# Between attention and experts: the order of the last two token tiles' routing, of the plan and of the first expert tiles

## The reference

```
h = tokenizer(x)                                   # 4 images x 256 tokens x 192
h = concatenate([h, txt])                          # 4 x 384 tokens x 192 = 1536 tokens
h = h + attention(layernorm(h))                    # softmax(-|q_n - q_m|^2 / 4) v, 12 heads, all 1536 x 1536
x = layernorm(h)
t = x / sqrt(mean(x*x) + eps) * norm_scale
g = t @ gate_w.T + gate_b                          # 16 logits for each token
top_vals, top_idx = top_k(g, 4)
comb = onehot(top_idx) weighted by softmax(top_vals)
u = t @ mlp1_w[e].T + mlp1_b[e]                    # 768 wide, pairs (glu, lin)
a = min(u_glu, 7) * sigmoid(1.702 * min(u_glu, 7)) * (clip(u_lin, -7, 7) + 1)
y = a @ mlp2_w[e].T + mlp2_b[e]
out = h + x + sum over the 4 experts of comb[e] * y[e]
```

## Time and profile before

| | |
|---|---|
| median of 3 runs | 739.37 us (733.47, 739.37, 743.79) |
| the profiled execution | 738.72 us |
| its span in the profile | 737.0 us |
| TensorE clock granted, mean of the span | 0.94 |
| busy: PE / PEld / DVE / ACT / POOL | 634.6 / 428.6 / 429.7 / 379.7 / 356.2 us |
| attention stage, about | 237 to 461 us |
| seam that the change touches, about | 461 to 498 us |
| expert stage, about | 489 to 724 us |

### The profile page before, as it was taken

The page is one execution under the profiler, slowest core; times in us unless marked ns, Lnnn a source line. Parts: engine busy times, 40 slices in busy tenths (PEclk is TensorE's granted clock), DMA queues, the critical chain, the costliest instruction groups (busy, mean ns, idle before and its releaser), DMA issues.

```text
span 737.0 us, 17256 instructions
## 1 busy us (share of the span) xinstructions
PE 634.6 (86%) x4926; PEld 428.6 (58%) x4927; DVE 429.7 (58%) x1430; ACT 379.7 (52%) x721; POOL 356.2 (48%) x401
## 2 busy tenths in 40 slices
PE   5888899888884999899999998549999999999970
PEld 5775786677641223222222223438999999999970
DVE  0347767676664235555555554537777777777750
ACT  0323438343312999988999898014344344344330
POOL 3112233222232125555555545514777787787781
PEclk9999999999985999999999999559999999999995
DMA  8999999400014426545555231059898999999834
GB/s 325 409 353 303 328 313 333 164 1 1 23 53 112 68 115 192 154 143 140 150 153 150 58 71 58 37 191 300 214 249 230 229 252 235 232 255 231 228 64 77
DMA packets 78192, 132.61 MB, mean 180 GB/s; under 512 B 36859, under 2 KB 62892, under 8 KB 76876
## 3 DMA queue, kind: packets, MB, share of 16 engines
q1 hardware_dynamic: 64892, 116.79, 50.7%
q0 software_dynamic: 11712, 14.19, 11.7%
q10 hardware_dynamic: 1552, 1.18, 0.5%
HBM read 105.53 MB, written 58.42 MB: 222 GB/s over the span
## 4 chain that ended last, share of the span: by engine, by line
PE 58%; DVE 10%; ACT 9%; DMA 8%; issue 6%; POOL 6%; another core or an unknown queue 1%; SPq 1%; ACTq 0%; DVEq 0%; POOLq 0%
PE ps L864 11%; PE ps L1015 9%; PE ps L851 9%; PE ps L1044 6%; PE ps L1025 5%; DMA odd_sum<-mid 4%; ACT big L1137 3%; ACT mid L1137 3%; PE ps L701 2%; PE ps L710 2%; POOL rstd L492 2%; DVE stat L1225 1%; DVE mid L1233 1%; PE ps L786 1%; DMA out<-mid 1%
## 5 line engine op out<-in xcount | busy, mean ns | idle before, releaser
L1137 ACT ACTIVATE mid<-ps 128x1536 f32<-128x1536 f32 x108 | 152.6, 1457 | 27.1 <-PE ps L851 26.3
L627 POOL TENSOR_TENSOR mid<-mid 128x384 f32<-128x384 f32 x63 | 81.2, 1289 | 53.2 <-DVE mid L1563 23.8
L851 PE MATMUL ps<-mid 52*128 52x512 f16 x432 | 88.0, 396 | 20.7 <-ACT big L1137 8.5
L1015 PE MATMUL ps<-mid,big 128*128 128x128 f32 x756 | 99.3, 282 | 0.3 <-ACT mid L1163 0.3
L1015 PEld LDWEIGHTS ps<-mid,big 128*128 128x128 f32 x756 | 91.5, 194 | 4.6 <-ACT mid L1163 0.5
L1554 DVE TENSOR_SCALAR mid<-ps,big 128x128 f32<-128x128 f32 x189 | 54.6, 344 | 62.0 <-PE ps L1025 34.7
L864 PE MATMUL ps<-mid 128*32 128x384 f32 x864 | 87.3, 507 | 0.0
L1170 ACT ACTIVATE mid<-mid 128x384 f32<-128x384 f32 x63 | 32.9, 522 | 88.4 <-DVE mid L1554 74.6
L1044 PE MATMUL ps<-big,mid 128*128 x378 | 71.0, 332 | 4.6 <-POOL mid L627 3.9
L851 PEld LDWEIGHTS ps<-mid 52*128 52x128 f16 x432 | 17.1, 95 | 85.8 <-ACT mid L1137 46.1
L1044 PEld LDWEIGHTS ps<-big,mid 128*128 128x128 f32 x378 | 60.1, 190 | 9.8 <-issue 9.6
(11 more groups left out here) (224 smaller groups left out, 1108.6 us busy)
## 6 DMA issues: line engine op xcount, KB each, us to landing
big<-w_cat SPq DMA_DIRECT2D x63, 576.0 KB
expert_in<-expert_in SPq DMA_DIRECT2D x16, 1774.5 KB, 48.4
big<-expert_in SPq DMA_DIRECT2D x63, 136.5 KB
w_cat<-w_a SPq DMA_DIRECT2D x4, 1536.0 KB, 7.6
big<-w SPq DMA_DIRECT2D x2, 2304.0 KB, 8.9
big<-patches SPq DMA_DIRECT2D x8, 512.0 KB, 8.8
big<-patches SPq DMA_DIRECT2D x2, 2048.0 KB, 21.9
w_cat<-w_b SPq DMA_DIRECT2D x2, 1536.0 KB, 7.5
```

What stands on the lines that cost most here:

```text
L627: nc.gpsimd.tensor_tensor(actv[r], prod[r], sig[r], ALU.mult).then_inc(actv_ready, 1)
L851: last = nc.tensor.matmul(SETS[kb % 2][:, c * 512:(c + 1) * 512], keysT[n_par][row:row + STK, kb * P:(kb + 1) * P], qrysT[n_par][row:row + ...
L1015: last = nc.tensor.matmul(banks[half][:, c * P:(c + 1) * P], w1_t[q][:, half * FF + c * P:half * FF + (c + 1) * P], xtT[r][:, 0:P], start= ...
L1137: nc.scalar.activation(probs[kb % 4], SETS[kb % 2], ACT.Exp, scale=0.5).then_inc(probs_ready, 1)
```

## The change

It touches only the order of things, and one job that is joined to another.

- DVE: `output(11)` comes before `weigh(10)`, and `norm_stats(11)` before `place(10)`.
- POOL: `route2` is split into `root_var` and `root_ms`. For the last two tiles: `root_var(11)`, the first scatter of tile 10, `root_ms(11)`, the scatters 1 and 2, `weights(11)`, the last scatter of tile 10, `base_add(11)`, the scatters of tile 11. Before, all four scatters stood between `route2(11)` and `weights(11)`.
- PE and DVE: the separate `counts` job is gone. The ranks job of tile 11 also computes the counts (as the seen tokens before tile 11 plus the mask of tile 11) beside the ranks in bank 7, and `place(11)` copies them out. All later job numbers are one lower.
- PE: `ranks(11)` comes before `weighted_bias(2)`; the plan's transposes come before `weighted_bias(4)` and `weighted_bias(5)`.
- SP: after the scatters have landed it issues rows 0, rows 1, weights 1, rows 2, weights 2, rows 3, weights 3; before, rows 0, weights 1, rows 1, weights 2, rows 2, weights 3, rows 3. Weights 0 go ahead of the wait in both.
- PE: the first products of tile 0 come before the transpose of tile 1.

```diff
             load_weights(0, 0)
             for k in range(2):
                 sp.wait_ge(rows_out[k], 16 * (TOPK * NT // 2 + 1))
-            for j in range(NW):
+            load_rows(0, 0)
+            for j in range(1, NW):
                 load_rows(j, j)
-                if j + 1 < NW:
-                    load_weights(j + 1, j + 1)
+                load_weights(j, j)
...
-            def route2(r):
+            def root_var(r):
                 held_wait(pool, lmv_ready, r + 1)
...
+            def root_ms(r):
                 held_wait(pool, ms_ready, r + 1)
...
-            def scatter(r, par):
+            def scatter(r, par, ks=range(TOPK)):
...
             weights(NT - 2)
             route(NT - 1)
-            route2(NT - 1)
-            scatter(NT - 2, 0)
+            root_var(NT - 1)
+            scatter(NT - 2, 0, (0,))
+            root_ms(NT - 1)
+            scatter(NT - 2, 0, (1, 2))
             weights(NT - 1)
+            scatter(NT - 2, 0, (3,))
             base_add(NT - 1)
             scatter(NT - 1, 1)
...
-            def ranks(r, job):
+            def ranks(r, job, counts=False):
...
-                nc.tensor.matmul(b7[:, 0:E], ones16[:], seen[:], start=False, stop=True).then_inc(tr_ready, 1)
-
-            def counts(job):
-
-                pe.wait_ge(tr_taken, job)
-                pe.wait_ge(slots_ready, NT)
-                nc.tensor.matmul(b7[:, 0:E], ones16[:], seen[:], start=True, stop=True).then_inc(tr_ready, 1)
+                last = nc.tensor.matmul(b7[:, 0:E], ones16[:], seen[:], start=False, stop=True)
+                if counts:
+                    nc.tensor.matmul(b7[:, E:2 * E], ones16[:], mask[:], start=True, stop=False)
+                    last = nc.tensor.matmul(b7[:, E:2 * E], ones16[:], seen[:], start=False, stop=True)
+                last.then_inc(tr_ready, 1)
...
             logits(base + 2)
+            ranks(NT - 1, base + 3, counts=True)
             weighted_bias(2)
-            ranks(NT - 1, base + 3)
             weighted_bias(3)
-            counts(base + 4)
+            pe.wait_ge(slots_ready, NT)
             for t in (NT - 2, NT - 1):
                 last = nc.tensor.transpose(ps[0:E, t * P:(t + 1) * P], comb_all[:, t, :], ident[:])
             last.then_inc(combT_psum, 1)
-            weighted_bias(4)
-            pe.wait_ge(combT_ready, 2)
-            weighted_bias(5)
-
-            pe.wait_ge(tr_taken, base + 5)
+            pe.wait_ge(tr_taken, base + 4)
             pe.wait_ge(plan_cols_ready, 1)
             for c in range(2):
                 last = nc.tensor.matmul(b7[0:1, c * P:(c + 1) * P], plan_cols[:, c:c + 1], ident[:], start=True, stop=True)
             last.then_inc(tr_ready, 1)
 
+            weighted_bias(4)
+            pe.wait_ge(combT_ready, 2)
+            weighted_bias(5)
+
...
             x_transpose(0, 0, 16)
+            mlp1(0, 0, 16)
             x_transpose(1, 1, 16)
-            two_tiles(0, 0, 0)
+            mlp1(1, 1, 16, narrow_first=True)
+            x_transpose(2, 2, 16)
+            x_transpose(3, 3, 16)
             two_tiles(2, 2, 0)
...
-            def place(r, par, job):
+            def place(r, par, job, counts=False):
 
                 dve.wait_ge(tr_ready, job + 1)
-                nc.vector.tensor_tensor(slot_e[:], b7[:, 0:E], bucket0[:], ALU.add).then_inc(tr_taken, 1)
+                last = nc.vector.tensor_tensor(slot_e[:], b7[:, 0:E], bucket0[:], ALU.add)
+                if counts:
+                    last = nc.vector.tensor_copy(cnt, b7[:, E:2 * E])
+                last.then_inc(tr_taken, 1)
...
             choose(NT - 2, base + 5)
-            weigh(NT - 2, 0)
             base += 7
             output(NT - 1, base - 1)
+            weigh(NT - 2, 0)
+            norm_stats(NT - 1, 1)
             place(NT - 2, 0, base)
-            norm_stats(NT - 1, 1)
             norm_square(NT - 1, 1)
...
-            place(NT - 1, 1, base + 3)
+            place(NT - 1, 1, base + 3, counts=True)
             dve.wait_ge(slots_ready, NT)
-
-            dve.wait_ge(tr_ready, base + 5)
-            nc.vector.tensor_copy(cnt, b7[:, 0:E]).then_inc(tr_taken, 1)
-            dve.wait_ge(tr_taken, base + 5)
             dve.wait_ge(plan_consts, 1)
```

More of the change, by code:

```diff
@@ L565, in weights @@
                 nc.gpsimd.tensor_tensor(wexp[:], euler[:], gd[:], ALU.pow).then_inc(wexp_ready, 1)
-            def scatter(r, par):
+            def scatter(r, par, ks=range(TOPK)):
                 held_wait(pool, slots_ready, r + 1)
-                for k in range(TOPK):
+                for k in ks:
                     nc.gpsimd.indirect_dma_start(
@@ L583, in pool_head @@
                 route(n - 1)
-                route2(n - 1)
+                root_var(n - 1)
+                root_ms(n - 1)
                 base_add(n - 1)
@@ L607, in _ @@
             weights(NT - 3)
-            route2(NT - 2)
+            root_var(NT - 2)
+            root_ms(NT - 2)
             base_add(NT - 2)
@@ L989, in _ @@
             last.then_inc(tr_ready, 1)
+            weighted_bias(4)
+            pe.wait_ge(combT_ready, 2)
+            weighted_bias(5)
             pe.wait_ge(w_in, 16 * 2)
             pe.wait_ge(plan_ready, 1)
-            pe.wait_ge(tr_taken, base + 6)
+            pe.wait_ge(tr_taken, base + 5)
             pe.wait_ge(bias_added, NT // 2)
@@ L1532, in _ @@
                                            ALU.add).then_inc(plan_cols_ready, 1)
-            dve.wait_ge(tr_ready, base + 6)
+            dve.wait_ge(tr_ready, base + 5)
             nc.vector.tensor_copy(ej_i, b7[0:1, 0:MT])
@@ L1536, in _ @@
             nc.vector.tensor_scalar(exrow_i, b7[0:1, 0:MT], float(P), None, ALU.mult).then_inc(tr_taken, 1)
-            dve.wait_ge(tr_taken, base + 6)
+            dve.wait_ge(tr_taken, base + 5)
             nc.vector.tensor_copy(bank_mark[:], ones[:, 0:1]).then_inc(plan_ready, 1)
```

## The result

The changed kernel takes 734.93 us (median of 20 runs, 730.38 to 741.98), the kernel before 740.74 (20 runs, 732.86 to 748.02). The ratio is 0.9947, 95% interval 0.9921 to 0.9972: about 3.9 us shorter, somewhere between 2 and 6. It is formed from the fast runs and is the measure used from here on; the two medians themselves lie 5.8 us apart, near the far end of that range. The forecast was 735.0 and 4.2 us.

The account below looks back on a forecast made before the run. TensorE bounds the later expert stage; the change shortens the wait chain ahead, about 460 to 500 us. Tile 1's products end 4.4 earlier, or 3.7; the sum is given as 4.2, so 735 us, range 729.5 to 741.5.

Parts of the forecast that it names:

- Output before weighing, roots and scatters: VectorE and GpSimd around tiles 10 and 11: the row of tile 11 is written from 467.1 instead of 467.94, 0.8 earlier.
- The 0.39 charged for a stall: Weighing tile 10 on VectorE: its first product is stretched under GpSimd's h_res add, from 0.23 to 0.62.
- the wider reading: Contention rule taken to cover scatters too: the square at 465.3 waits 0.9 for the first scatter; sum 0.8 smaller.
- I charge scatters nothing: VectorE beside GpSimd's scatters: GpSimd adds stretch two-input products, but scatters are given no cost.
- The power: GpSimd's power of tile 11, formerly behind four scatters of tile 10: runs from 470.7 instead of 473.14, 2.4 earlier.
- the scatters' landing: DMA of tile 11's four scatters: follows the slots rigidly and lands at 481.7 instead of 484.18.
- The plan: Plan and first weight issue come 3.4 earlier, at 479.9; no gain by itself, as SP waits for scatters until 481.7.
- Row load 0: First row load, issued by SP at 482.5: takes 3.2 (bounds 2.5 to 3.9), landing at 485.7.
- Products of tile 0: TensorE, ahead of tile 1's transpose: start at 486.9 instead of 492.03; tile 1's products end 4.4 earlier, or 3.7.
- Rival B: Part is given back: half clock through tile 1 (+1.9) or row loads gain nothing; 2.3 remain, 736.5; chance 0.20.
- The DMA of h_res ... shifts with it: ScalarE's transfer of h_res into out, awaited by GpSimd's first add: issued behind copy 3 and shifts with it.
- The conveyor: Later expert stage, TensorE busy 99.91 of 100 us at full clock: an earlier first tile should make the end earlier.

Follow-up runs that it names:

- plan_only: The kernel before with only the counts inside the ranks job and the plan's transposes ahead of the last bias products; ratio to before 0.9983 (0.9949 to 1.0018).
- start_only: The kernel before with only the new order of loads and tile 0's products ahead of tile 1's transpose; ratio to before 0.9975 (0.9946 to 1.0005).
- undo_sp: The changed kernel with the old order of loads (weights 1 ahead of rows 1, and so on); ratio to before 0.9968 (0.9930 to 1.0006).
- slots_only: The kernel before with only VectorE's new order and tile 10's scatters in pieces around the two powers; ratio to before 0.9957 (0.9924 to 0.9989).
- gate_loose: The changed kernel with GpSimd's product of tile 3 ahead of the first indirect add, later products likewise; ratio to before 0.9948 (0.9909 to 0.9986).
- gate_old_start: The changed kernel with GpSimd's product of tile 3 ahead of the first add and both start edits taken back; ratio to before 0.9951 (0.9915 to 0.9987).
- undo_pe: The changed kernel with TensorE's old start order, transposes of tiles 0 and 1 before tile 0's products; ratio to before 0.9982 (0.9946 to 1.0018).
- warm: The changed kernel with 11 unread products on TensorE behind the last bias products, before the first rows; ratio to before 0.9995 (0.9951 to 1.0040).
- out_mid: The changed kernel with the h_res transfer issued behind ScalarE's copies of tiles 0 and 1; ratio to before 0.9944 (0.9902 to 0.9986).

## Why the prediction was right

The time, its sign and its size were right. Step by step, counted from the last output copy:

- **Output before weighing, roots and scatters:** the row of tile 11 was forecast 0.8 earlier and came 1.3 earlier (8.1 to 6.8). The 0.39 charged for a stall didn't occur: VectorE's product began at 458.33, GpSimd's add at 458.43, and the product took 0.22. The Trainium skill's "SBUF — State Buffer", section "Who interferes with whom", says that issue order decides which of the two blocks; the trace agrees as far as the product, 0.1 ahead, wasn't held, while the add behind it took 0.59, as in the earlier trace rows, so that it was blocked can't be seen. The square at 461.50 took 0.36 inside the scatter of 461.26 to 462.42, as before (466.24), so the wider reading doesn't hold for it. But "I charge scatters nothing" was too simple: one step of weighing, L1467, took 0.48 at 468.72, inside the scatter of 468.19 to 469.23, and took 0.23 before; in all eleven kernels with the new slots it took 0.48 there. What singles it out among VectorE's steps beside scatters is open. What I charged for the held root, 0.1 to 0.3, was 0.14 (its input stood at 462.32 with the usual 0.08, it began 462.46).
- **The power,** the largest term: 2.4 forecast, 2.9 measured (13.3 to 10.4); **slots** 2.5 and 2.9; **the scatters' landing** 2.5 and 3.3 (24.4 to 21.1), as the last piece landed in 2.91 and not 3.21. The stall of placing under the base add was small (0.33 for 0.22), where up to 0.39 was charged.
- **The plan** earlier gains nothing on its own: right for the issue of row load 0, which in `plan_only` is where it was.
- **Row load 0** lands in 2.8 (478.44 to 481.25); I took 3.2.
- **Products of tile 0:** 5.1 forecast, 6.4 measured, but tile 0 takes 4.5 and not 3.5, and the pause 1.1 and not 0.7, since the products of tile 0 and the transpose behind them lie at half clock: tile 1's end 4.4 forecast, 4.1 measured. Rival B's half clock through tile 1 did not come here; it came in `start_only` and `undo_sp`.
- **"The DMA of h_res ... shifts with it"** is the term that was wrong. It was issued 4.3 earlier and took 1.0 longer, beside loads that were themselves brought forward, and tile 3's product waits for it. At tile 4 the lead was 4.5, at tile 6 3.3; against the end of tile 1 it is 0.8 lost.
- **The conveyor,** on which an earlier first tile makes an earlier end, held for these two kernels (222.7 and 222.6 from tile 6 on). Over all fourteen profiles that stretch differed by up to 4.7.

So the sum of 4.2 (the working gives 4.4, or 3.7 with a slower load, and doesn't say how it comes to 4.2) is near 3.4 (profile) and 3.9 (runs) because terms that were too small and others that were too large cancel, and that is luck. The mechanism of the slots was right. What the sum got wrong is who earned it. It put 1.9 of the 4.4 at tile 1's end on the start edits (2.5 on the slots); `slots_only` alone has tile 6 at 50.9, the whole change at 51.2. In the whole change the lead of the start edits is spent on the half clock and on the h_res gate. That this is all they are ever worth is not shown: `gate_loose` against `gate_old_start` leaves them 1.4.

## What to carry to other kernels

Between two stages, move the issue of a slow queue behind the small operation that others wait for: four scatters, 1.27 to 1.53 us apart, stood ahead of one power, and the reordering around them had as much as the whole change. When the first operations of the next stage are brought forward, look for the next wait that all of them share (here a transfer whose landing one engine's order puts ahead of another's work), and count what moves forward with it on the same DMA engines. An earlier start with a pause in it can bring less than nothing at tile 2 (`start_only`: 2.9 ahead at tile 0, 0.8 behind at tile 2, at half clock throughout), and an idle 2 us later on costs its own length and then some half clock (`undo_pe`, `warm`). And when one wait is taken away, look at what binds next before counting the gain: `out_mid` and `gate_loose` open the gate in two ways, and both stop at tile 6 at 49.5.

## What was not expected of the hardware

- From the first product on the half clock lasted 9.2 us in `start_only` and 8.9 in `undo_sp`, both with one pause of 1.1 us between products of which 0.47 is idle, and 4.5 to 5.2 us in the five other profiles with that pause. Without it it was 2.6 to 3.4 in four profiles (`slots_only`, `undo_pe`, before, `plan_only`) and 5.2 in `gate_old_start`. So the pause goes with a longer half clock in these profiles, but what decides between 5 and 9 us, or between 3 and 5, is open.
- The same 1152 KB transfer of h_res took 7.5 to 12.0 us in these fourteen kernels. What was loaded beside it differed; that this is the reason was not tested.
- In both kernels with the 11 unread products, the last scatter of tile 11 landed 4.3 to 4.4 us after its issue instead of 2.9 in the changed kernel (2.8 to 3.3 in the others), and row load 0 was issued at 23.3 to 23.4 instead of 21.8 to 22.3 as in the others with the new slots; the chain of waits of `warm`:

```profile
478.96 4.37 DMA expert_in<-big,slot_u
```

  TensorE and scatters share nothing that the profile shows. What delays them is open.
